# A transformer block on one core: the first layer norm moves from the token layout to the column layout

## What is computed

```python
B, L, C, H, D, FF = 32, 256, 288, 16, 18, 1152
ada = silu(cond) @ W_ada + b_ada           # six vectors of 288 per batch: shift, scale, gate, twice
h = layernorm(x) * (1 + scale_msa) + shift_msa        # eps 1e-6
qkv = h @ W_qkv + b_qkv                    # 16 heads of 18
o = softmax(q @ k.T * D**-0.5) @ v         # per batch and head, 256 x 256 scores
x = x + gate_msa * (o @ W_proj + b_proj)
h = layernorm(x) * (1 + scale_mlp) + shift_mlp
x = x + gate_mlp * (gelu(h @ W_fc1 + b_fc1) @ W_fc2 + b_fc2)
```

## Time and profile before

| | us |
|---|---|
| median of 3 runs | 1234.8 (1233.38 to 1235.49) |
| the profiled execution: its own time | 1228.32 |
| the profiled execution: span from first to last instruction | 1226.5 |
| PE busy | 1181.1 |
| DVE busy | 901.8 |
| ACT busy | 866.1 |
| POOL busy | 540.3 |

### The profile page before, as it was taken

The page is one execution under the profiler, slowest core; times in us unless marked ns, Lnnn a source line. Parts: engine busy times, 40 slices in busy tenths (PEclk is TensorE's granted clock), DMA queues, the critical chain, the costliest instruction groups (busy, mean ns, idle before and its releaser), DMA issues.

```text
span 1226.5 us, 27564 instructions
## 1 busy us (share of the span) xinstructions
PE 1181.1 (96%) x9863; PEld 1064.3 (87%) x9863; DVE 901.8 (74%) x1928; ACT 866.1 (71%) x1485; POOL 540.3 (44%) x557
## 2 busy tenths in 40 slices
PE   6888999999999999999999999999999999999977
PEld 5666999999998999999999999999999999997777
DVE  5687777877777787778777777777777787775553
ACT  5387777777777777777777777777777777778721
POOL 3012544444454444445454444444444445443364
PEclk9799999999999999999999999999999999999999
DMA  8554555554555554445555444555554555444220
GB/s 265 171 169 138 167 167 164 164 154 144 163 160 159 168 166 145 157 157 162 167 166 164 147 159 150 166 165 167 161 153 148 158 166 159 162 149 140 87 68 20
DMA packets 134330, 188.91 MB, mean 154 GB/s; under 512 B 24544, under 2 KB 102422, under 8 KB 133947
## 3 DMA queue, kind: packets, MB, share of 16 engines
q1 hardware_dynamic: 134033, 186.71, 48.3%
q10 hardware_dynamic: 162, 0.44, 0.1%
HBM read 121.92 MB, written 64.63 MB: 152 GB/s over the span
## 4 chain that ended last, share of the span: by engine, by line
PE 84%; SPq 5%; DMA 4%; DVE 3%; ACT 2%; issue 1%; POOL 0%; ACTq 0%; POOLq 0%; DVEq 0%
PE a_bank L867 10%; PE x_bank L785 10%; PE score_bank L808 9%; PE turn_bank L834 9%; PE st_bank L822 9%; PE b_bank L867 8%; PE b_bank L881 6%; PE b_bank L882 5%; PE b_bank L883 5%; PE a_bank L848 4%; PE x_bank L793 4%; SPq L623 2%; DMA qk_rows<-qst 1%; DMA ql<-zeros 1%; PE x_bank L759 1%
## 5 line engine op out<-in xcount | busy, mean ns | idle before, releaser
L1138 DVE TENSOR_REDUCE mx<-score_bank 128x2 f32<-128x512 f32 x512 | 342.0, 687 | 95.8 <-PE score_bank L808 93.7
L953 ACT ACTIVATE e<-st_bank 128x1024 f32<-128x1024 f32 x256 | 262.4, 1025 | 125.8 <-PE st_bank L822 123.5
L1287 POOL TENSOR_TENSOR gl<-gl_raw,gh 128x512 fp32r<-128x512 f32 (+1 forms) x160 | 194.3, 1221 | 226.4 <-DVE gh L1203 226.4
L946 ACT CAST ql<-mxt 4x256 fp32r<-4x256 f32 x512 | 206.2, 403 | 7.4 <-DVE mxt L1147 0.6
L808 PEld LDWEIGHTS score_bank<-kl,ql 122*128 122x128 f32 x1024 | 146.9, 190 | 42.0 <-issue 24.4
L808 PE MATMUL score_bank<-kl,ql 122*128 122x256 f32 x1024 | 174.6, 293 | 5.6 <-DMA ql<-zeros 3.3
L881 PE MATMUL b_bank<-w,gh 128*128 128x288 f32 x576 | 174.5, 303 | 2.2 <-DVE tmp L1209 1.9
L822 PE MATMUL st_bank<-ql,kl 122*128 122x512 f32 x512 | 165.7, 405 | 7.7 <-ACT e L953 6.9
L882 PE MATMUL b_bank<-w,gh 128*128 128x288 f32 x576 | 170.5, 296 | 0.0
L883 PE MATMUL b_bank<-w,gl 128*128 128x288 f32 x576 | 170.3, 296 | 0.0
L834 PE MATMUL turn_bank<-e,ve 128*32 128x256 f32 x2048 | 123.8, 382 | 0.3 <-ACT e L953 0.3
(11 more groups left out here) (152 smaller groups left out, 2473.1 us busy)
## 6 DMA issues: line engine op xcount, KB each, us to landing
qk_rows<-qst SPq DMA_DIRECT2D x128, 256.0 KB, 5.3
ql<-qk_rows SPq DMA_DIRECT2D x384, 72.0 KB
kl<-qk_rows SPq DMA_DIRECT2D x378, 72.0 KB
o_rows<-on SPq DMA_DIRECT2D x128, 128.0 KB
gate<-gates SPq DMA_DIRECT2D x32, 432.0 KB, 4.4
xin<-in_x SPq DMA_DIRECT2D x32, 288.0 KB, 5.9
x<-in_x SPq DMA_DIRECT2D x32, 288.0 KB, 3.0
out<-x SPq DMA_DIRECT2D x32, 288.0 KB, 4.5
```

The source lines that it names most:

```text
L946: last = nc.scalar.copy(rows[:, :, :, t, a, :], src)
L953: nc.scalar.activation(e[:, j % 4, :, :, :].rearrange("p u i l -> p (u i l)"), st_bank[:, :, :, :].rearrange("p u i l -> p (u i l)"), ACT. ...
L1138: nc.vector.tensor_reduce(mx[:, j // HP, i, :, col:col + 1], score_bank[i][:, :].rearrange("p (t l) -> p t l", t=NT), AX.X, ALU.max).then_ ...
L1287: nc.gpsimd.tensor_tensor(gl[:, cols], g[:, cols], gh[:, cols].bitcast(F32), ALU.subtract).then_inc(g_lo, 1)
```

## The change

**The first layer norm without transposes.** The host hands over a second copy of x, `in_x_turned`: for each batch 3 x 128 x 256, channels on the partitions, tokens along the row, with the last 32 channels four times. It is loaded into `xt_in` (384 KB a batch). The statistics are still taken with tokens on the partitions from `xin`, which has one buffer now. Mean and rstd of each token (`mr1`, 128 x 2 x 2) are written to DRAM, 2 KB in pieces of 8 bytes, and read back as one row of 512 numbers into all 128 partitions (`mrow`, 256 KB). DVE subtracts the mean and multiplies with rstd in two instructions over 128 x 768, in place; ACT applies scale and shift from `xt_in`. The six transposes of `xt` on PE are gone, and with them two of the seven fillings of `x_bank`. The second layer norm is as before.

**The start.** x of batch 0 is loaded directly behind the conditioning vector, and DVE takes its statistics ahead of the copies that feed `mod_columns(0)`. The moments of batch 0 are written and read by ACT, around the rounding of the first weight. PE does products of `wq` with itself into `score_bank1`, which nothing reads: ten behind `mod_columns(0)`, one in each of three places and four ahead of the first scores, each 512 columns wide. `second_mod` and two gate products stand ahead of the first scores now.

**Orders anew.** All tables of all five engines are new, the repeated ones and those of the ends. POOL's copy of the batch's scale and shift is a step of its own (`mod1`). SP has three new steps: `xc` (load `xt_in`), `mw` (write moments), `mr` (read them into all partitions).

```diff
-X_USES = 2 + QK_PARTS + NT
-USE_QK, USE_V = 2, 2 + QK_PARTS
+LN1 = 5
+X_USES = QK_PARTS + NT
+USE_QK, USE_V = 0, QK_PARTS
...
 SYNC_ORDER = [
-    ("qkr", 0, 10), ("qkr", 0, 11), ("or", -2, 1), ("qkr", 0, 12), ("or", -2, 2), ("or", -2, 3), ("store", -4, 0),
...
+    ("rr", -2, 3), ("qkr", 0, 21), ("mw", 2, 0), ("qkw", 1, 0), ("sr", -1, 0), ("qkr", 0, 22), ("qkr", 0, 23),
+    ("or", -2, 5), ("qkr", 0, 24), ("qkr", 0, 25), ("mr", 2, 0), ("qkw", 1, 1), ("ln1_stats", 3, 0), ("rr", -2, 4),
...
-        xin = sb("xin", [P, 2, NT, C])
-        xn = sb("xn", [P, NT, CX])
+        xin = sb("xin", [P, NT, C])
+        xt_in = sb("xt_in", [P, 3, L])
+        mrow = sb("mrow", [P, L, 2])
...
+        def m_places(b):
+
+            return m_dram[b % 2].rearrange("(t p) s -> p t s", p=P), mr1[:, :, :]
+
+        def m_spread(b):
+
+            return (mrow[:, :, :].rearrange("p l s -> p (l s)"),
+                    m_dram[b % 2].rearrange("l s -> (l s)").unsqueeze(0).broadcast_to([P, 2 * L]))
...
+            def fetch_columns(b):
+                wait(sp, x1_mod, 2 * b)
+                sp.dma_start(xt_in[:, :, :], x_turned[b]).then_inc(xt_loaded, 16)
+
+            def store_m(b):
+                sp.wait_ge(rstd1, b + 1)
+                if b >= 2:
+                    sp.wait_ge(m_rows, 16 * (b - 1))
+                sp.dma_start(*m_places(b)).then_inc(m_stored, 16)
+
+            def spread_m(b):
+                sp.wait_ge(m_stored, 16 * (b + 1))
+                wait(sp, ln1_dve, LN1 * b)
+                sp.dma_start(*m_spread(b)).then_inc(m_rows, 16)
...
+            def warm(_b, n):
+                for _ in range(n):
+                    nc.tensor.matmul(score_bank[1][:, :], wq[:, 0, 0:P], wq[:, 0, 0:2 * L], start=True, stop=True)
+
+            pe.wait_ge(w_hi, 1)
+            warm(0, 10)
+
...
-            def xt(b, n):
-                pe.wait_ge(ln1_dve, 4 * b + 4)
-                wait(pe, x_drained, X_USES * b + n)
-                turn_x(x_bank, xn, n).then_inc(x_full, 1)
-
...
-            for i in range(N_FIRST):
+            act.wait_ge(rstd1, 1)
+            nc.scalar.dma_start(*m_places(0)).then_inc(m_stored, 16)
+            round_weights(0)
+            act.wait_ge(m_stored, 16)
+            nc.scalar.dma_start(*m_spread(0)).then_inc(m_rows, 16)
+            for i in range(1, N_FIRST):
                 round_weights(i)
...
+                row = mrow[:, :, t].unsqueeze(1).broadcast_to([P, 3, L])
+                nc.vector.tensor_tensor(xt_in[:, :, :], xt_in[:, :, :], row, (ALU.subtract, ALU.mult)[t]
+                                        ).then_inc(ln1_dve, 1)
```

More of the change, by code:

```diff
@@ L399, in dit_block @@
         gates_stored = sem("gates_stored")
-        x_loaded = sems("x_loaded", 2)
+        x_loaded = sem("x_loaded")
+        xt_loaded = sem("xt_loaded")
+        m_stored = sem("m_stored")
+        m_rows = sem("m_rows")
+        x1_mod = sem("x1_mod")
         ln1_dve = sem("ln1_dve")
@@ L539, in _, with fetch_x @@
         def _(sp):
+            def fetch_x(b):
+                wait(sp, ln1_dve, LN1 * (b - 1) + 1)
+                sp.dma_start(xin[:, :, :], x[b].rearrange("(p t) c -> p t c", t=NT)).then_inc(x_loaded, 16)
+            def fetch_columns(b):
[10 more added lines that the diff above has]
+                sp.dma_start(*m_spread(b)).then_inc(m_rows, 16)
             sp.dma_start(c_in, cond).then_inc(c_loaded, 16)
+            fetch_x(0)
             def load_ada(cols, done):
@@ L568, in load_weights, with x_columns, m_write, m_read @@
                                  w[k * P:(k + 3) * P, :].rearrange("(f p) c -> p f c", p=P)).then_inc(w_loaded[i], 16)
-            def fetch_x(b):
-                wait(sp, ln1_dve, 4 * b - 4)
-                sp.dma_start(xin[:, b % 2], x[b].rearrange("(p t) c -> p t c", t=NT)).then_inc(x_loaded[b % 2], 16)
             def ln1_stats(b, _):
-                if b >= 2:
+                if b:
                     fetch_x(b)
+            def x_columns(b, _):
+                if b:
+                    fetch_columns(b)
+            def m_write(b, _):
+                if b:
+                    store_m(b)
+            def m_read(b, _):
+                if b:
+                    spread_m(b)
             def res(b, _):
@@ L916, in xt @@
                     wait(act, x1_rem, b)
-                act.wait_ge(x_full, X_USES * b + n + 1)
+                    wait(act, x_full, X_USES * b)
+                act.wait_ge(ln1_dve, LN1 * (b + 1))
                 for c in (0, 1) if n == 0 else (2,):
                     rows = P if c < 2 else KR
-                    last = nc.scalar.activation(v1[0:rows, c, :], x_bank[0:rows, (c % 2) * L:(c % 2 + 1) * L],
+                    last = nc.scalar.activation(v1[0:rows, c, :], xt_in[0:rows, c, :],
                                                 ACT.Identity, bias=mod1[0:rows, c:c + 1], scale=mod1[0:rows, 3 + c:4 + c])
-                last.then_inc(x_drained, 1)
+                last.then_inc(x1_mod, 1)
             def qk(b, n):
@@ L1007, in _, with ln1_moments @@
         def _(dve):
+            def ln1_moments(b):
+                dve.wait_ge(x_loaded, 16 * (b + 1))
+                for t in range(NT):
+                    last = nc.vector.bn_stats(stat1[:, t, :], xin[:, t, :])
+                last.then_inc(ln1_dve, 1)
+                dve.wait_ge(ln1_dve, LN1 * b + 1)
+                for t in range(NT):
+                    last = nc.vector.bn_aggr(mv1[:, t, :], stat1[:, t, :])
+                last.then_inc(ln1_dve, 1)
+                dve.wait_ge(ln1_dve, LN1 * b + 2)
+                wait(dve, m_stored, 16 * b)
+                nc.vector.tensor_tensor(mr1[:, :, :], mv1[:, :, :], eps1[:, :, :], ALU.add).then_inc(ln1_dve, 1)
             nc.vector.memset(mod[:, :, :], 0.0)
@@ L1103, in gates @@
                 nc.vector.tensor_tensor(gate_val[:, 2, :], gate_val[:, 1, :], b_fc2_row, ALU.mult).then_inc(gates_ready, 1)
-            first_stats()
             for i in range(N_FIRST):
                 split_weights(i)
-            for t in range(NT):
-                normalise(xin[:, 0], mv1, rs1, xn, ln1_dve, rstd1, 0, t)
             modulation(0)
@@ L1119, in xt @@
             def xt(b, n):
[L1120 removed]
+                dve.wait_ge(x1_mod, 2 * b + n + 1)
                 if n == 0:
@@ L1337 @@
     args.append(nc.dram_tensor("zeros", (HP, 2 * HP * L), F32, kind="Internal").ap())
+    args.append(nc.dram_tensor("m_rows", (2, L, 2), F32, kind="Internal").ap())
+    turned = np.asarray(inputs["x"]).reshape(B, P, NT, C).transpose(0, 3, 2, 1).reshape(B, C, L)
+    rows = list(range(2 * P)) + list(range(2 * P, C)) * (P // REM)
+    turned = np.ascontiguousarray(turned[:, rows].reshape(B, 3, P, L).transpose(0, 2, 1, 3))
+    arrays["in_x_turned"] = turned
+    args.append(nc.dram_tensor("in_x_turned", turned.shape, mybir.dt.from_np(turned.dtype), kind="ExternalInput").ap())
     dit_block(nc, *args)
```

201 lines of the change are left out of this document (105 added, 96 removed), and 186 rows, old and new, of tables (ACT_HEAD, ACT_ORDER, ACT_TAIL, DVE_HEAD).

## The result

The forecast was 1213.3 us (1203 to 1227). The changed kernel took 1305.5 us in the median of 4 runs (1301.5 to 1309.3), against 1234.1 for the kernel before: a ratio of 1.058 (95% interval 1.054 to 1.063), 71 us slower. It was measured in two more series, beside the experiments: 1283.1 us (ratio 1.040, 1.037 to 1.043) and 1281.6 us (1.038, 1.034 to 1.041), where the kernel before stayed at 1233.5 and 1235.1. So the change costs 47 to 71 us, where the forecast had a gain of 21.5.

A forecast was written before the change was run, and what follows sets the result against it. PE alone was taken to set the pace from 120 to 1100 us. The terms, 18.5 + 3 + 0 + 0 = 21.5 us gained, gave a forecast of 1213.3 us, range 1203 to 1227.

The forecast's parts named there:

- Rival C: SP becomes the bound: the small write lands so late that `mr` holds the queue; near 1240 us; 7 in 100.
- term 2: Start: moments' trip delays the first projection, clock and new order regain more; 3 us gained, bounds loss of 4, gain of 10.
- rival A: Start: the trip through DRAM makes the first scores 4 us later, nothing regained; time 1220 us; 12 in 100.
- The credit for the clock: Start, PE: unread products keep the clock up, gaining 1.5 us in batch 0's projections and 3.3 around the first scores.
- Term 1: Middle, PE: dropping the first layer norm's transposes saves 0.66 us a batch, 18.5 us over 28 batches.
- Term 4: Middle, PE: the new order switches at other places; 0 us taken, bounds 3 us better and 8 worse over 27 periods.
- Term 3: End, last 126 us: same chain in nearly the same order; 0 us, bounds 3 us either way.
- the signs of being wrong: Period over 35.3, PE waiting for q and k every batch, clock 0.5 at first scores, or first scores behind 44 us.

The follow-up runs named there:

- the best kernel: Changed kernel with moments on ACT, no unread products, batch 0 by transposes, earlier moments' steps, later fc2 loads and `o_rows` reads: 1228.8 us, 0.995 of the kernel before.

## Why the prediction was wrong

**The step that failed first is SP's: the price of the small write's landing, and the rest that was to absorb it.** I priced the write of the moments as the write of the sums, "3.4 us in the median, 4.9 at most", and wrote that the wait is "0 in the median and up to 1.3 us", and that 1.8 + 1.3 is "still under 4.5". The write landed 6.1 us after its issue (5.4 in the later series), and SP waited 50.3 us in 24 periods, 2.1 us each. The seven issues in between were priced right: in the period that the chain above is taken from they end 3.6 us behind the start of the write. The 2.0 us that the prediction quotes from the Trainium skill beside its own price are further off still. The skill's "DMA: Bandwidth & Descriptors", Anatomy of one DMA, gives that fit for transfers that GpSimd issues, and this write was issued by SP; the measured 5.4 to 6.1 us decide.

Nor was SP's rest something that could be spent anywhere. Without the trip SP still had 89 us of waits for other engines in the same 900 us, 3.5 a period. Two issues and this wait, 2.9 a period, would fit in by the sum, and yet between the two marks a batch takes 2.1 us more with the trip (1058.8 against 998.0 us). An average of rest says nothing of the place; the moved `mr`, which only lays five issues into the wait, brought 29 us back.

"What is new is that SP waits for a landing" is wrong as well. It waited 18.7 us for `o_rows` before, which the earlier trace rows leave out, and I had no step for those landings. The landing of the write of the sums went from 3.4 us to 5.3, and `rr` waits for it 23.0 us. In the kernel without the trip it lands after 4.7, so most of that comes with the new order and the load of `xt_in`, which that kernel keeps.

**Rival C happened,** with 7 in 100 and the right mechanism, but its sums are wrong twice. Its threshold adds the 0.66 us of the transposes to SP's 4.5 us of rest. A shorter period leaves SP less rest, so they are to be taken off: 1.8 + (landing - 3.6) passes 3.84 at a landing of 5.6 us, not 7. And "27 us worse at the middle's end" is against the kernel before, so 8 us mean 1259, with the 3 us of the start taken off; 1240 is the 27 added to the forecast, which holds the transposes' gain already. Even with the right sign the rule is too mild: it has no loss at 5.4 us and a small gain left at 6.1, where the changed kernel lost 47 and 71 us (its start included), because it lets the wait draw on the whole rest.

**The second failed step is in term 2, and with it rival A happened (12 in 100), larger than it was priced:** first scores 9.8 us later, not 4. Term 2 priced the moments' write in the start at 3.4 to 4.9 us and the read at 5.6, and put the first projection at 21.5. They took 10.6 and 7.7, beside the weights' loads with all DMA engines busy (a share of 0.97 from 15 to 30 us), and it started at 30.08. The rows that I used come from the middle and from behind the weights. The nearest rows in place, not in kind, were the transfers of the first 20 us of the kernel before: those in flight from 7 to 20 us landed 6.6 to 9.5 us after their issue, one of 36 KB after 7.1. Taking batch 0 off the trip moved the projection to 18.55 and gave 11.9 us. The bounds of the term (a loss of 4) didn't hold it: 12.9 us were lost by the mark at batch 3 with the trip in batch 0 alone, 25.3 with all, so the trips of the next batches cost about as much again.

**The credit for the clock in term 2 fell.** Nothing came of the 1.5 us, nor of the 3.3 at the scores; the clause "if PE does not idle between" was the point, and it idles for 10.4 us. From 60 to 120 us the clock was even lower than before (0.79 against 1.00). Whether unread products that fill the whole gap would have held it, no run shows.

**Term 1 was right in size.** 0.66 us a batch predicted, 0.65 measured by doubling, though without the 0.17 that the term had put on the two switches. **Term 4** was not nothing: with no wait left the period is 35.2 and not 35.0. The 0.2 us a batch, 6 us in all, are within its bound of 8; that the order takes them is what remains, not what a run shows. **Term 3** was right: 0.5 us less behind the last mark. **DVE's** two products took 0.97 us (1.0 predicted), but its other lines grew so that it works more and not less: 788 us of 900 without the trip, 696 before (see the last section). It wasn't the bound. Of the signs of being wrong three came: a period over 35.3 (37.5), half a clock at the first scores, and first scores behind 44 us.

Put together: the transposes' 0.65 us a batch less these 0.2 are about 12 us gained in the middle (12.4 without the trip, by the two marks), and they show only where no queue is held by the trip. Even the best kernel loses about as much at the start (its mark at batch 3 stands 14.1 us late), and its 0.5% come with two edits that the change doesn't contain.

## What to carry to other kernels

A transfer that a queue must wait for, where the queue takes its issues in order, is priced by its landing at its own place, under the load there and in its own piece size; then look at which issues can be laid between it and its reader, and move the reader or put it on a queue of an engine with rest. Rest in a queue's total is no allowance: ask at each place what is behind the wait. And here a detour through DRAM cost nothing only where the pipeline was full and the wait for it well placed; the first batch did better the old way.

## What the hardware showed

A 2 KB write in 256 pieces of 8 bytes landed in 5.3 to 6.1 us in the median among others at a DMA share of 0.6, and in 10.6 us in the start with all DMA engines busy; 128 pieces of 16 bytes landed in 3.3 us. The Trainium skill, "DMA: Bandwidth & Descriptors", Queues, rings and completion order, says that the increment of a semaphore lands only behind every earlier write of the same DMA engine, over all its queues; the 10.6 us on ACT's otherwise empty queue agree with that, but no run here isolates it.

DVE's products of two tensors became slow where POOL works beside them. The smallest one, 32 x 256, by source in the changed kernel (ns minimum/median/maximum), and one of them on DVE's timeline:

```profile
L1185 DVE TENSOR_TENSOR xr<-xl_raw,xr x64: 416/1395/1544, 30.3 to 1278.0; 32x256 fp32r<-32x256 f32 x64
```

```profile
478.19 0.58 DVE L1190 CAST xh<-xl_raw 128x512 fp32r<-128x512 f32 x1
478.69 0.89 DVE L1182 CAST xr<-xl_raw 96x256 fp32r<-96x256 f32 x1
479.62 1.40 DVE L1185 TENSOR_TENSOR xr<-xl_raw,xr 32x256 fp32r<-32x256 f32 x1
```

POOL's own product (line 1335) started at 479.40 for 1.34 us, and DVE's ended 0.28 us behind it. Before, DVE's product began after POOL's was over (508.14 against 506.67 + 1.29), and the line took 0.42 us in the median. Together with two like lines (1235 and 1241) it took 122.8 us from 200 to 1100 us, where the same three took 45.0 before. In the kernel without the trip PE is busy for 899.95 of 900 us all the same, so the slower products hold nobody up there. The Trainium skill, "SBUF — State Buffer", Who interferes with whom, says that a DVE instruction with two inputs in SBUF contends with a GpSimd (here POOL) instruction that reads SBUF, and that one of the two then waits until the other is done; the trace agrees, with 1.40 us instead of 0.42.

In the kernel with batch 0 by transposes a DVE product with scalars over 288 columns took 4.47 us (7.96 to 12.43) beside two memsets of POOL (7.87 to 12.26), and 0.42 right behind them.
